# Pre-norm attention layer with a sign-weight layer: second normalisation folded into centred signs and a row scale, first normalisation as scale and bias on ACT, bias row begun one step sooner

## The reference, cut to what matters

```python
def _layernorm(x, axis=-1, eps=1e-05):
    m = jnp.mean(x, axis=axis, keepdims=True)
    v = jnp.var(x, axis=axis, keepdims=True)
    return (x - m) / jnp.sqrt(v + eps)

def attn(x):                                  # x is already normalised
    q, k, v = x @ Wq.T + bq, x @ Wk.T + bk, x @ Wv.T + bv      # split in 16 heads
    scores = where((j <= i) & (j >= i - 128), q @ k.T * 0.25, -10000.0)
    a = softmax(scores) + 1e-09
    return (a @ v) @ Wo.T + bo

x = x + attn(_layernorm(x))
x = x + _layernorm(x) @ sign(weight).T
```

## Time and profile before

| | us |
|---|---|
| runs | 905.56, 903.35, 894.11 |
| median | 903.35 |
| the profiled execution | 896.96 |
| its span, first to last instruction | 895.2 |
| mean granted PE clock | 0.926 of full |

### The profile page before, as it was taken

The page is one execution under the profiler, slowest core; times in us unless marked ns, Lnnn a source line. Parts: engine busy times, 40 slices in busy tenths (PEclk is TensorE's granted clock), DMA queues, the critical chain, the costliest instruction groups (busy, mean ns, idle before and its releaser), DMA issues.

```text
span 895.2 us, 31506 instructions
## 1 busy us (share of the span) xinstructions
PE 744.8 (83%) x13072; PEld 617.3 (69%) x13072; DVE 638.8 (71%) x1171; ACT 484.2 (54%) x1029; POOL 453.1 (51%) x582
## 2 busy tenths in 40 slices
PE   2668888888898888889888888988888898888874
PEld 1657777767777777667776677777776687776663
DVE  7565767778777677877778687776877866776643
ACT  1346655546656455665556466565656555455630
POOL 7235455556536445554546465465545544545641
PEclk9788999889999899999999899999999988899995
DMA  3787656566567476664557754665667734677310
GB/s 100 104 100 106 100 95 116 98 114 99 105 100 109 82 117 115 102 111 85 102 108 107 110 104 99 94 112 89 112 114 120 108 74 93 95 105 106 67 37 18
DMA packets 104190, 87.94 MB, mean 98 GB/s; under 512 B 11441, under 2 KB 104049, under 8 KB 104049
## 3 DMA queue, kind: packets, MB, share of 16 engines
q1 hardware_dynamic: 102112, 84.49, 57.6%
q10 hardware_dynamic: 1936, 1.45, 0.5%
HBM read 18.22 MB, written 8.39 MB: 30 GB/s over the span
## 4 chain that ended last, share of the span: by engine, by line
PE 48%; DVE 32%; issue 11%; POOL 3%; ACT 2%; SPq 2%; DMA 1%; DVEq 0%; POOLq 0%; ACTq 0%
PE gc L837 16%; DVE nmax L694 9%; PE sc L965 9%; PE pv L983 8%; PE ga L837 7%; DVE xn L651 6%; PE mx L924 2%; POOL rs L434 2%; DVE st L635 2%; PE mx L931 2%; PE ga L994 2%; PE gb L1006 2%; DVE st L785 2%; DVE k_lo L682 2%; ACT k_hi L498 2%
## 5 line engine op out<-in xcount | busy, mean ns | idle before, releaser
L536 ACT ACTIVATE prob<-sc 128x512 f32<-128x512 f32 x448 | 263.5, 595 | 223.8 <-PE sc L965 220.1
L965 PE MATMUL sc<-q_stack,k_stack 128*128 128x256 f32 (+1 forms) x1024 | 229.4, 316 | 14.0 <-ACT prob L536 11.0
L694 DVE TENSOR_REDUCE nmax<-mx 128x6 f32<-128x960 f32 x188 | 194.7, 1036 | 5.4 <-PE mx L931 4.2
L965 PEld LDWEIGHTS sc<-q_stack,k_stack 128*128 128x128 f32 x1024 | 159.0, 197 | 52.4 <-issue 30.3
L419 POOL TENSOR_SCALAR_AFFINE_SELECT prob<-prob 128x1024 f32<-128x1024 f32 x128 | 154.9, 1210 | 0.0
L983 PE MATMUL pv<-prob,v_ones 128*32 128x128 f32 x3840 | 150.6, 285 | 0.1
L432 POOL TENSOR_SCALAR ve<-mv 128x1 f32<-128x1 f32 x64 | 14.0, 219 | 261.7 <-DVE mv L789 261.7
L661 DVE SCALAR_TENSOR_TENSOR xn<-x,mv,rs 128x256 f32<-128x256 f32 x64 | 81.4, 1272 | 63.4 <-POOL rs L434 63.4
L416 POOL TENSOR_SCALAR_AFFINE_SELECT prob<-prob 128x1024 f32<-128x1024 f32 x112 | 122.8, 1096 | 7.5 <-ACT prob L536 7.5
L983 PEld LDWEIGHTS pv<-prob,v_ones 128*32 128x32 f32 x3840 | 95.9, 112 | 27.7 <-issue 4.2
L674 DVE SCALAR_TENSOR_TENSOR q_lo<-gc,bq,q_hi 128x256 fp32r<-128x256 f32 x64 | 28.0, 480 | 83.1 <-ACT q_hi L487 83.1
(11 more groups left out here) (136 smaller groups left out, 1572.1 us busy)
## 6 DMA issues: line engine op xcount, KB each, us to landing
q_stack<-q_hi SPq DMA_DIRECT2D x128, 128.0 KB, 3.8
k_stack<-k_hi SPq DMA_DIRECT2D x128, 128.0 KB, 4.6
xs<-x SPq DMA_DIRECT2D x32, 256.0 KB, 4.4
q_stack<-q_lo SPq DMA_DIRECT2D x64, 128.0 KB, 4.6
k_stack<-k_lo SPq DMA_DIRECT2D x64, 128.0 KB, 4.8
xr<-x SPq DMA_DIRECT2D x64, 128.0 KB, 2.1
out<-x SPq DMA_DIRECT2D x64, 128.0 KB, 3.4
q_max<-q SPq DMA_DIRECT2D x64, 64.0 KB
```

The costliest lines, as they stand in the source:

```text
L536: a.activation(prob[:, own:nxt + 1:nxt - own, 2 * f:2 * f + 2, :], sc, ACT.Exp, scale=SCALE).then_inc(exp_done, 1)
L694: v.tensor_reduce(nmax[:, n % 2, :].rearrange("p (r h) -> p r h", r=C)[:, :, h0:h0 + m], banks[:, :, 0:WIN * m].rearrange("p r (h k) -> p ...
L965: last = mm(sc_bank[f % 2][:, 2 * P * j:2 * P * j + q], k_stack[:, h, ak:ak + P], q_stack[:, h % HB, P * t:P * t + q], start=True, stop=True)
```

## The change

The second normalisation is no longer carried out on x2. With s the sign matrix, r the reciprocal root and m the mean of a row, (x2 - m) r s = r (x2 (s - mean of s)). So PE turns x2 itself, `w_sign` is centred once (PE sums its columns with a matrix of ones, DVE subtracts), and the last sum on DVE becomes product times `rs2` plus x2. `norm2` and `xn2` are gone, and `turn_x2` waits for x2. The first normalisation moves from DVE to ACT as scale times x plus bias, with the bias -m r made by two more small operations on POOL; its place is between exp 6 and the copy of `u` in even steps. `stats1` moves forward on DVE, to behind `normalise`. `sum_bias` moves ahead of the third group of maxima in step 2, and in step 3 POOL adds the bias row after the first masking.

```diff
 # POOL, rsqrt1
                 g.tensor_tensor(rs1[:, :], ve1[:, :], half[:, :], ALU.pow).then_inc(rs1_done, 1)
+                g.tensor_scalar(nm1[:, :], mv1[:, :, 0], -1.0, None, ALU.mult).then_inc(nm1_done, 1)
+                pool.wait_ge(rs1_done, n + 1)
+                pool.wait_ge(nm1_done, n + 1)
+                g.tensor_tensor(nmr1[:, :], nm1[:, :], rs1[:, :], ALU.mult).then_inc(nmr1_done, 1)
...
 # POOL, slot
-                if part["op"]:
+                if part["op"] and t != 3:
                     add_biases(*part["op"])
                 if part["ln"]:
                     rsqrt1(*part["ln"])
                 if now:
                     mask_probs(*now, 0)
+                if part["op"] and t == 3:
+                    add_biases(*part["op"])
...
 # ACT
+            def norm1(b, p):
+                i, _ = halves(p)
+                n = PAIRS * b + p
+                act.wait_ge(nmr1_done, n + 1)
+                wait(act, t1_filled, n)
+                for j in range(2):
+                    last = a.activation(xn[:, j], xs[:, i, j], ACT.Identity, bias=nmr1[:, j:j + 1], scale=rs1[:, j:j + 1])
+                last.then_inc(xn_done, 1)
...
                 if part["tqv"]:
                     q_16_part(*part["tqv"])
+                if part["ln"]:
+                    norm1(*part["ln"])
                 if part["pv"]:
...
             w_part("q")
+            for p in range(2):
+                norm1(0, p)
             xt_part(0, 0, sc_bank[0])
...
                 k_16_part(0, p)
+            norm1(0, 2)
             xt_part(0, 2, pv_bank)
...
 # DVE, slot
-                if part["ff"]:
-                    norm2(*part["ff"])
                 if part["mx"]:
                     row_max(*part["mx"], 0)
                 if part["op"]:
                     normalise(*part["op"])
+                if part["ln"]:
+                    stats1(*part["ln"])
...
                     dve.wait_ge(ff_filled, TILES * bb + tt + 1)
-                    v.tensor_tensor(x2[:, i], ga[:, 0:D], x2[:, i], ALU.add).then_inc(y_done, 1)
+                    dve.wait_ge(rs2_done, TILES * bb + tt + 1)
+                    v.scalar_tensor_tensor(x2[:, i], ga[:, 0:D], rs2[:, i:i + 1], x2[:, i], ALU.mult, ALU.add).then_inc(y_done, 1)
...
                     row_max(*part["mx"], 2)
-                if part["ln"]:
-                    norm1(*part["ln"])
...
+                if now and (b, t) == (0, 0):
+                    centre_signs()
...
+            def centre_signs():
+                dve.wait_ge(sign_filled, 1)
+                for c in range(C):
+                    last = v.scalar_tensor_tensor(w_sign[:, c, :], ga[:, 0:D], -1.0 / D, w_sign[:, c, :].bitcast(F32),
+                                                  ALU.mult, ALU.add)
+                last.then_inc(w_sign_done, 1)
...
 # PE
             def turn_x2(b, t, later):
-                pe.wait_ge(xn2_done, n + 1)
+                pe.wait_ge(x2_done, n + 1)
...
-                    last = nc.tensor.transpose(gb[:, P * c:P * (c + 1)], xn2[:, P * c:P * (c + 1)], ident[:, :])
+                    last = nc.tensor.transpose(gb[:, P * c:P * (c + 1)], x2[:, t % 2, P * c:P * (c + 1)], ident[:, :])
...
+            def sum_signs():
+                pe.wait_ge(v_done, 3)
+                for c in range(C):
+                    last = mm(ga[:, 0:D], ones[:, :], w_sign[:, c, :].bitcast(F32), start=c == 0, stop=c == C - 1)
+                last.then_inc(sign_filled, 1)
...
                     q_proj(*tqv, 1)
+                if now and t == 2:
+                    sum_bias(b)
                 if mx:
                     max_scores(*mx, 2)
                 if pv:
                     prob_v(*pv, 2)
                 if now:
                     scores(b, t, 6)
-                if now and t == 2:
-                    sum_bias(b)
                 if op:
                     out_proj(*op)
+                if now and (b, t) == (0, 0):
+                    sum_signs()
```

More of the change, by code:

```diff
@@ L86, in build @@
         rs1 = sb("rs1", [P, 2])
+        nm1 = sb("nm1", [P, 2])
+        nmr1 = sb("nmr1", [P, 2])
         xn = sb("xn", [P, 2, D])
@@ L125, in build @@
         ve2 = sb("ve2", [P, 1])
-        rs2 = sb("rs2", [P, 1])
-        xn2 = sb("xn2", [P, D])
+        rs2 = sb("rs2", [P, 2])
         t2_hi = sb("t2_hi", [P, C, P], F32R)
@@ L166, in build @@
         bn1_done, mv1_done, ve1_done, rs1_done, xn_done = map(sem, ("bn1_done", "mv1_done", "ve1_done", "rs1_done", "xn_done"))
+        nm1_done, nmr1_done = sem("nm1_done"), sem("nmr1_done")
         t1_filled, xt_hi_done, xt_lo_done = map(sem, ("t1_filled", "xt_hi_done", "xt_lo_done"))
@@ L183, in build @@
         op_filled, xb_done, x2_done, bn2_done, mv2_done = map(sem, ("op_filled", "xb_done", "x2_done", "bn2_done", "mv2_done"))
-        ve2_done, rs2_done, xn2_done = map(sem, ("ve2_done", "rs2_done", "xn2_done"))
+        ve2_done, rs2_done, sign_filled = map(sem, ("ve2_done", "rs2_done", "sign_filled"))
         t2_filled, t2_hi_done, t2_lo_done = map(sem, ("t2_filled", "t2_hi_done", "t2_lo_done"))
@@ L433, in rsqrt2 @@
                 pool.wait_ge(ve2_done, n + 1)
-                g.tensor_tensor(rs2[:, :], ve2[:, :], half[:, 0:1], ALU.pow).then_inc(rs2_done, 1)
+                g.tensor_tensor(rs2[:, t % 2:t % 2 + 1], ve2[:, :], half[:, 0:1], ALU.pow).then_inc(rs2_done, 1)
             def slot(b, t):
@@ L641, in stats1 @@
                 last.then_inc(mv1_done, 1)
[L643 to L662, removed]
             def xt_part(b, p, bank=gc):
@@ L750, in slot @@
                     row_max(*part["mx"], 1)
-                if part["ln"]:
-                    stats1(*part["ln"])
                 if part["op"]:
@@ L786, in slot @@
                     dve.wait_ge(bn2_done, n + 1)
-                    wait(dve, xn2_done, n)
+                    wait(dve, ve2_done, n)
                     v.bn_aggr(mv2[:, :], st2[:, :]).then_inc(mv2_done, 1)
+                if now and (b, t) == (0, 0):
+                    centre_signs()
             def split_w(i, n):
@@ L794, in split_w @@
                                 ALU.subtract).then_inc(w_lo_done, 1)
+            def centre_signs():
[4 more added lines that the diff above has]
+                last.then_inc(w_sign_done, 1)
             for p in range(2):
                 stats1(0, p)
-                norm1(0, p)
             split_w(0, "q")
@@ L807, in _ @@
             xt_part(0, 1, sc_bank[1])
-            norm1(0, 2)
             q_part(0, 1)
@@ L1029, in second_layer @@
                 pe.wait_ge(t2_lo_done, n + 1)
+                if n == 0:
+                    pe.wait_ge(w_sign_done, 3)
                 if later:
```

## The result

The changed kernel takes 820.11 us (median; 817.36 to 821.44), against 903.88 for the kernel before, run beside it. The ratio is 0.909, with a 95% interval of 0.902 to 0.916. In a second comparison it was 820.27 against 901.19, 0.906 (0.897 to 0.914). The ratios leave out executions in a slower state, with a lower granted clock, so a ratio need not be the quotient of two medians. The forecast was 824, from 790 to 866.

The account below looks back on a forecast made before the run. PE and DVE take turns, PE waiting mainly for norm2 at turn_x2. Span 895.2 - 75.0 + 24.4 + 3.7 - 4.5 - 23 = 820.8 us, with 1.8 around it 822.6, stated as 824; range 790 to 866.

Parts of the forecast that it names:

- The bound: PE and DVE take turns; PE waits at turn_x2 behind norm1, the POOL round trip and norm2, 54.2 us in 34 waits.
- What is removed, 75.0: PE's waits that go: 54.2 us at turn_x2, 11.2 for row maxima, 9.6 for cx.
- norm1 on ACT, 24.4: norm1 behind exp 6 lands on PE: 0.84 us in each of 29 pairs, 24.4 us added, 36.5 at the bound.
- the upper bound: norm1's two ACT instructions take at most 1.26 us a pair, 36.5 us over 29 pairs.
- Covered parts: POOL's small operations, the longer last sum on DVE, and the moved stats1 and sum_bias cost nothing.
- Prologue and end: Prologue and centring add 3.7 us together; the last steps, behind 880, gain 4.5 us with the gaps.
- Clock: Shorter PE waits bring back half of the 46 us lost at half clock: 23 us gained.
- The first: Low clock stays, or the wait for exp 7 calls as many low stretches as norm2: 847 us, chance 0.20.
- The second: Late exp 7 delays ACT and DVE; PE waits at turn_c and second_layer: 874 us, chance 0.12.
- The third: Slower: all idle time returns at other waits and exp 7 costs 0.84 us a pair: 925 us, chance 0.05.
- The fifth: Early bias row: cx still late in step 3 behind spread_bias, 9.6 us stay: 833 us; shares the forecast's 0.55.

Follow-up runs that it names:

- the fold alone: Kernel before with only the second normalisation folded into centred signs and row scale, norm1 and bias row at their old places: 795.76 us, ratio 0.882.
- the first two experiments: Kernel before with only norm2 folded into the signs and row scale, 795.76 us; kernel before with only norm1 moved to ACT, 841.67 us.

## Why the prediction was right

**The bound.** Right: PE waited for DVE at `turn_x2`, and the waits went. The reasons given were `norm1` ahead of x2 and `norm2` behind its round trip. Neither makes the waits alone: either one taken off DVE ends them. What the prediction didn't ask is whether the second edit was worth its price. At the place behind exp 6 it was not: the fold alone takes 795.76 us, some 24 less than the change on the same chip. Ahead of exp 6 it was, with 775.36.

**What is removed, 75.0.** The waits at `turn_x2` are gone, 13.9 us for the maxima are left (15.7 forecast), and 0.4 of 9.6 for `cx`. That makes 76.4 us less. The 13.9 is partly the work of `sum_bias`'s new place, which the prediction put at nothing: with the bias row at its old place there are 18.1 us, 60 to 740. The waits for `cx` were right in size and only half right in cause: not `norm2` alone, but either normalisation on DVE makes `cx` late, as the first two experiments showed.

**norm1 on ACT, 24.4.** The two instructions take 1.08 us, not 0.84; the upper bound was 1.26. The wait grew from 0.34 and 0.41 to 1.27 and 1.40, and its sum from 11.0 to 38.2 us, 27 more. The group of `norm1` in the changed kernel:

```profile
L488 ACT ACTIVATE xn<-xs,nmr,rs 128x256 f32<-128x256 f32 x64 | 34.6, 590 | 9.7 <-POOL nmr L399 9.7
```

One takes 590 ns against 471 with one row scalar, 119 more. The Trainium skill (ScalarE: Activation LUTs, What ACT_TABLE_LOAD costs) gives some 93 ns for each such operand, and was nearer than the row that I took. `norm1` also reads SBUF, which was not tried apart.

**Covered parts.** The small operations take 0.24 and 0.19 us on POOL, and end 3 us ahead of `norm1`: right.

```profile
416.63 0.19 POOL L399 TENSOR_TENSOR nmr<-nm,rs 128x2 f32<-128x2 f32 x1
```

The last sum takes 475 ns (480 forecast), hidden. The bias row is worth nothing, right.

**Prologue and end.** 2.5 lost for 2.7 forecast. The end gained 11.3, of which the forecast had 4.5 and the 3.8 in the waits between 862 and 880, 8.3: low by 3. It had no term for the clock there, and the granted clock was 0.65 from 862 to 895 before and is 0.86 from 793.3 to 815.6 now.

**Clock.** From 0.94 over 760 us to 0.96 over 685: 91 us at half clock before, 2 x 0.04 x 685 = 55 after, so 36 less and up to 18 gained, for 23 forecast. The wait of 1.27 did call low stretches, 16 of them from 60 to 745, where `norm1` ahead of exp 6 leaves the mean at 1.00. So the whole price of `norm1`'s place is 45 us, as the move ahead of exp 6 shows. The forecast had it in two terms, 24.4 of waits and 23 of clock not given back, 47 together.

**The sum.** 76.4 - 27 - 2.5 + 18 + 7.5 (the end without the 3.8 that are in the waits) makes 72 of the 79.6 us measured. The other 7 are not accounted for term by term; smaller waits fell as well, those for `t_lo` from 3.9 to 1.1. That the forecast of 824 lies only 4 us from 820.11 is in part luck: the price on ACT and the clock's gain were too favourable by 3 and 5 us, the end and the small waits not favourable enough.

**The rivals.** The first, that the low clock stays as it is, didn't come: 36 us less at half clock. The second (the gain taken back behind `turn_x2`) didn't come: 1.1 us of waits for `t_lo`. The third needed more than 0.6 us a pair beyond the waits removed; even twice the work at this place ended 2% under the kernel before. The fifth (`cx` late behind `spread_bias`) didn't come either: 0.4 us is left.

## What to carry to other kernels

When a step is moved to an engine with idle time, look at the instructions right behind its new place: an engine at 54% busy can be without slack at one place of the step and have 1.8 us of it one instruction earlier. Price a new wait of PE with what it does to the clock, and measure two edits that remove the same wait apart, since their gains don't add, and one of them may cost more than it adds. SP issued its copies in order: a copy whose source was late, moved to the front, held up all that stood behind it for some 3 us.

## What the runs showed that was not expected

An element-wise DVE instruction on an SBUF tensor with one tensor input was held up beside POOL's maskings like the one with two (median 1162 ns, least 412; it ended 0.14 to 0.15 us behind the masking, the other 0.27 to 0.28). Statistics over an equal tile were not held up beside POOL's additions (406 to 419 ns). Instructions with one of their tensor inputs in PSUM were not held up beside a masking either: the last sum of the changed kernel takes 473 to 477 ns in 44 such cases, 474 to 484 without. The granted clock answered more than in proportion: waits of 0.30, 1.27 and 2.25 us, four to a batch, went with mean clocks of 1.00, 0.96 and 0.90. At 1.27 us a low stretch (0.50, 1.2 GHz) followed 16 of the 28 waits up to 745 us.
